# Moving four operands of VectorE from SBUF to PSUM, with three PSUM banks for the groups' sums in place of six

## The reference, cut to what matters

```python
edge_emb = edge_attr_full @ ew.T + eb
xw = x @ W
xj = xw[src].reshape(-1, H, D) + edge_emb.reshape(-1, H, D)
xi = xw[dst].reshape(-1, H, D)
alpha = einsum('ehd,hd->eh', xi, att_i) + einsum('ehd,hd->eh', xj, att_j)
alpha = leaky_relu(alpha, 0.2)
amax = segment_max(alpha, dst, num_segments=N)
ea = exp(alpha - amax[dst])
denom = segment_sum(ea, dst, num_segments=N)
msg = xj * (ea / (denom[dst] + EPS))[..., None]
h = segment_sum(msg, dst, num_segments=N).mean(axis=1) + b     # then relu, next layer
```

## Time and profile before

| | value |
|---|---|
| median of 3 runs | 3343.92 us |
| time of the profiled execution | 3336.89 us |
| its span, first to last instruction | 3335.0 us |
| mean granted clock of TensorE | 0.543 |
| busy: PE, POOL, DVE, ACT | 72%, 65%, 61%, 20% |

### The profile page before, as it was taken

One profiled execution on the slowest core, in us unless ns is written; L12 is line 12 of the kernel. 1 busy time (PEld: TensorE's weight loads), 2 busy tenths in 40 slices (PEclk: granted clock), 3 DMA queues, 4 the chain that ended last, 5 costly groups with the idle time before them and its releaser, 6 DMA issues.

```text
span 3335.0 us, 48601 instructions
## 1 busy us (share of the span) xinstructions
PE 2402.9 (72%) x13595; PEld 1979.9 (59%) x13595; DVE 2021.6 (61%) x6441; ACT 669.5 (20%) x3102; POOL 2172.8 (65%) x2357
## 2 busy tenths in 40 slices
PE   6879955777675677668477777747777685777668
PEld 6669924566564566556366565636556573556557
DVE  8965464665565565656655665755665574665557
ACT  0048921111114111110411111131111122111112
POOL 0047737777755777774677777377777737777772
PEclk9555555555557555555755555575555566555556
DMA  3211112222221222221222222122222212222221
GB/s 100 102 66 68 46 55 59 60 61 58 63 48 43 58 63 58 58 64 40 50 63 58 58 67 56 33 59 61 58 60 64 56 35 57 60 60 58 58 55 50
DMA packets 114123, 195.78 MB, mean 59 GB/s; under 512 B 39898, under 2 KB 77273, under 8 KB 113865
## 3 DMA queue, kind: packets, MB, share of 16 engines
q0 software_dynamic: 62560, 130.25, 17.4%
q1 hardware_dynamic: 51304, 62.42, 5.9%
HBM read 180.86 MB, written 11.67 MB: 58 GB/s over the span
## 4 chain that ended last, share of the span: by engine, by line
POOL 30%; DVE 28%; PE 22%; issue 13%; DMA 4%; DVEq 2%; ACT 1%; POOLq 0%; ACTq 0%
POOL ring L510 28%; PE bank L745 10%; PE bank L747 5%; DMA ring<-table,srci 4%; DVE acc L1208 2%; PE bank L718 2%; DVE into L1149 2%; PE bank L741 2%; DVE prod L1072 2%; DVE ring L847 2%; DVE lanes L1135 2%; DVE fwd L1156 1%; POOL ring L491 1%; PE bank L783 1%; DVEq L1016 1%
## 5 line engine op out<-in xcount | busy, mean ns | idle before, releaser
L510 POOL DMA_INDIRECT ring<-table,srci x1955 | 1903.9, 974 | 633.1 <-issue 571.4
L745 PE MATMUL bank<-pw,ring 128*128 128x48 f32 x3910 | 1216.9, 411 | 0.0
L745 PEld LDWEIGHTS bank<-pw,ring 128*128 128x128 f32 x3910 | 1009.1, 316 | 103.8 <-issue 23.9
L741 PE MATMUL bank<-zeros 128*128 128x288 bf16 x490 | 209.6, 428 | 622.0 <-DVE pw L1167 622.0
L747 PE MATMUL bank<-onehot,est 128*36 128x24 f32 x3910 | 619.1, 246 | 0.0
L747 PEld LDWEIGHTS bank<-onehot,est 128*36 128x36 f32 x3910 | 382.6, 150 | 177.5
L586 ACT ACTIVATE dd<-dd 128x66 f32<-128x66 f32 x75 | 19.4, 258 | 2152.2 <-DVE dd L1160 2152.2
L741 PEld LDWEIGHTS bank<-zeros 128*128 128x128 bf16 x490 | 54.3, 111 | 665.3 <-DVE pw L1167 630.7
L1111 DVE TENSOR_TENSOR alpha<-alpha,ring 128x56 f32<-128x56 f32 (+7 forms) x75 | 18.1, 241 | 702.6 <-DMA ring<-table,srci 702.4
L1208 DVE TENSOR_TENSOR acc<-acc,bank 128x288 f32 x490 | 222.4, 454 | 301.7 <-PE bank L747 183.0
L580 ACT COPY ai_win<-ai_rows 128x48 f32 x1955 | 309.1, 228 | 58.0 <-issue 22.7
(11 more groups left out here) (214 smaller groups left out, 2676.1 us busy)
## 6 DMA issues: line engine op xcount, KB each, us to landing
ring<-table,srci POOLq DMA_INDIRECT x1955
ai_rows<-lo_dram SPq DMA_DIRECT2D x28, 896.0 KB, 4.3
at<-in_attr SPq DMA_DIRECT2D x65, 224.0 KB, 2.5
table<-ring SPq DMA_DIRECT2D x15, 390.0 KB, 3.6
table<-ring SPq DMA_DIRECT2D x5, 325.0 KB, 3.3
result<-ring SPq DMA_DIRECT2D x24, 64.0 KB
x_mid<-ring SPq DMA_DIRECT2D x3, 384.0 KB, 2.7
table<-ring SPq DMA_DIRECT2D x5, 130.0 KB, 2.3
```

The lines of the kernel that those rows point to most:

```text
L510: nc.gpsimd.indirect_dma_start(out=ring[:, slot(t), :], out_offset=None, in_=table, in_offset=bass.IndirectOffsetOnAxis(ap=srci[:, t:t + 1 ...
L741: nc.tensor.matmul(total, zeros[:, 0:P], zeros[:, :], start=True, stop=False, skip_group_check=True)
L745: nc.tensor.matmul(wide[:, 0:H, at_k], ring[:, slot(t), 0:D], pw[:, g % DEEP, k, :, :], start=False, stop=False, skip_group_check=True)
```

## The change

Four operands of DVE move into PSUM, and a few instructions are merged:

- `ai_win` lies in banks 4 to 6. ACT writes it there, and DVE multiplies it in place by `onehot`, now with one TENSOR_TENSOR of 1344 elements instead of two SCALAR_TENSOR_TENSOR of 672.
- `probs`, the layer's edge vectors `v16` and the dot rows `dot_row` lie in bank 7. The products of attributes become one TENSOR_TENSOR of 896 elements each instead of two of 448. `weigh` reads `probs` instead of the copy in `est`.
- The group sums keep banks 0 to 2, `pw` has three buffers, and `AHEAD` is 3.
- The node rows at a layer's start go through bank 6 alone.
- A copy of `vrow` into `dot_row` (once a layer, after chunk 10) and one of `v17` into `v16` (at a layer's start) are added.

```diff
-AHEAD = 4
-SUM_BANKS = (0, 1, 2, 4, 5, 6)
+AHEAD = 3
+SUM_BANKS = (0, 1, 2)
...
-        bank = [ctx.enter_context(nc.psum_tensor(f"bank{i}", [P, 512], F32)) for i in range(8)]
+        banks = ctx.enter_context(nc.psum_tensor("banks", [P, 8 * 512], F32))
+        bank = [banks[:, i * 512:(i + 1) * 512] for i in range(8)]
+        ai_win = banks[:, 4 * 512:4 * 512 + K * H * WIN].rearrange("p (k h w) -> p k h w", k=K, h=H)
+        dot_row = bank[7][:, 0:H * D].rearrange("p (h f) -> p h f", h=H)
+        probs = bank[7][:, H * D:H * D + H * QB].rearrange("p (h k) -> p h k", h=H)
+        v16 = bank[7][:, H * (D + QB):H * (D + QB + FA)].rearrange("p (h f) -> p h f", h=H)
...
-                if q >= 2:
-                    pe.wait_ge(tr_sb, NQ * layer + q - 1)
+                if q >= 1:
+                    pe.wait_ge(tr_sb, NQ * layer + q)
...
-                    nc.tensor.transpose(bank[6 + q % 2][:, o:o + P], xt[:, j, 0:D], identf[:, :]).then_inc(tr_ps, 1)
+                    nc.tensor.transpose(bank[6][:, o:o + P], xt[:, j, 0:D], identf[:, :]).then_inc(tr_ps, 1)
...
+            def layer_rows(layer):
+                v.wait_ge(lay_w, 16 * 5 * (layer + 1))
+                link(V.tensor_copy(dot_row, vrow[:, :, :]))
...
-                V.tensor_tensor_reduce(out=dump[:, d % NDUMP, :], in0=xt[:, j, 0:D], in1=vrow[:, h, :], scale=1.0,
+                V.tensor_tensor_reduce(out=dump[:, d % NDUMP, :], in0=xt[:, j, 0:D], in1=dot_row[:, h, :], scale=1.0,
...
-                    for h in range(H):
-                        ins = V.scalar_tensor_tensor(out=pr[:, h, :, :], in0=at[:, gc % NAT, 0:k, :], scalar=1.0,
-                                                     in1=v17[:, layer, h, 0:FA].unsqueeze(1).broadcast_to((P, k, FA)),
-                                                     op0=ALU.mult, op1=ALU.mult)
-                    link(ins)
+                    link(V.tensor_tensor(pr, at[:, gc % NAT, 0:k, :].unsqueeze(1).broadcast_to((P, H, k, FA)),
+                                         v16.unsqueeze(2).broadcast_to((P, H, k, FA)), ALU.mult))
...
-                    for h in range(H):
-                        ins = V.scalar_tensor_tensor(out=win[:, :, h, :], in0=win[:, :, h, :], scalar=1.0,
-                                                     in1=onehot[:, ts, :], op0=ALU.mult, op1=ALU.mult)
-                    link(ins)
+                    link(V.tensor_tensor(win, win, onehot[:, ts, :].unsqueeze(2).broadcast_to((P, k, H, WIN)), ALU.mult))
...
-                                est[:, c % 2, k:k + n, HF:HF + H].unsqueeze(3).broadcast_to((P, n, H, WIN)), ALU.mult)\
+                                probs[:, :, k:k + n].rearrange("p h k -> p k h").unsqueeze(3).broadcast_to((P, n, H, WIN)),
...
-                for h in range(H):
-                    ins = V.scalar_tensor_tensor(out=es[:, :, h * FA:(h + 1) * FA], in0=at[:, gc % NAT, 0:k, :], scalar=1.0,
-                                                 in1=probs[:, h, 0:k].unsqueeze(2).broadcast_to((P, k, FA)),
-                                                 op0=ALU.mult, op1=ALU.mult)
-                ins.then_inc(est_ready, 1)
+                V.tensor_tensor(es[:, :, 0:HF].rearrange("p k (h f) -> p k h f", h=H),
+                                at[:, gc % NAT, 0:k, :].unsqueeze(2).broadcast_to((P, k, H, FA)),
+                                pr.unsqueeze(3).broadcast_to((P, k, H, FA)), ALU.mult).then_inc(est_ready, 1)
...
+                V.tensor_copy(v16, v17[:, layer, :, 0:FA])
...
+                            layer_rows(layer + 1)
```

More of the change, by code:

```diff
@@ L122, in program @@
         at = sb("at", [P, NAT, K, FA])
-        ai_win = sb("ai_win", [P, K, H, WIN])
+        w2b2 = sb("w2b2", [P, 2 * D])
         prod = sb("prod", [P, H * K * FA])
@@ L136, in program @@
         dd = sb("dd", [P, H * QB + REG])
-        probs = sb("probs", [P, H, QB])
         maxes = sb("maxes", [P, H, QB])
@@ L258, in program @@
         iota_rep = estf[:, 0:P * PC // 2].bitcast(BF16).rearrange("p (l t) -> p l t", l=P)
-        w2s = ai_win[:, :, :, :].rearrange("p k h w -> p (k h w)")[:, 0:D]
-        b2s = ai_win[:, :, :, :].rearrange("p k h w -> p (k h w)")[:, D:2 * D]
-        bank = [ctx.enter_context(nc.psum_tensor(f"bank{i}", [P, 512], F32)) for i in range(8)]
+        w2s, b2s = w2b2[:, 0:D], w2b2[:, D:2 * D]
+        banks = ctx.enter_context(nc.psum_tensor("banks", [P, 8 * 512], F32))
[4 more added lines that the diff above has]
+        v16 = bank[7][:, H * (D + QB):H * (D + QB + FA)].rearrange("p (h f) -> p h f", h=H)
         def gcn_sum(g):
@@ L599, in old_rows @@
                     nc.scalar.copy(S[:, j0:j1, D:2 * D],
-                                   bank[6 + q % 2][:, 0:(j1 - j0) * P].rearrange("p (j n) -> p j n", n=P)).then_inc(tr_sb, 1)
+                                   bank[6][:, 0:(j1 - j0) * P].rearrange("p (j n) -> p j n", n=P)).then_inc(tr_sb, 1)
                 for q in range(NQ):
@@ L1062, in _ @@
             v.sem_inc(ln_coef, 1)
-            v.wait_ge(lay_w, 16 * 5)
+            def layer_rows(layer):
+                v.wait_ge(lay_w, 16 * 5 * (layer + 1))
+                link(V.tensor_copy(dot_row, vrow[:, :, :]))
+            layer_rows(0)
             dots = [0]
@@ L1168, in weigh @@
                                 onehot[:, t:t + n, :].unsqueeze(2).broadcast_to((P, n, H, WIN)),
-                                est[:, c % 2, k:k + n, HF:HF + H].unsqueeze(3).broadcast_to((P, n, H, WIN)), ALU.mult)\
+                                probs[:, :, k:k + n].rearrange("p h k -> p k h").unsqueeze(3).broadcast_to((P, n, H, WIN)),
+                                ALU.mult)\
                     .then_inc(p_ready, 1)
@@ L1175, in chain_probs @@
                 v.wait_ge(exp_al, gc + 1)
-                link(V.transpose(probs[:, :, :], dd[:, 0:H * QB].rearrange("p (h e) -> p h e", h=H)))
+                link(V.transpose(probs, dd[:, 0:H * QB].rearrange("p (h e) -> p h e", h=H)))
                 pr = probs[:, :, 0:k].rearrange("p h k -> p k h")
@@ L1298, in _ @@
                     v.wait_ge(xmid_in, 16)
-                else:
-                    v.wait_ge(lay_w, 16 * 5 * (layer + 2))
                 for j in range(NT):
```

## The result

The changed kernel takes **3272.35 us**, the median of 4 runs (3267.82 to 3273.49), against 3344.14 us for the kernel before (4 runs): a ratio of 0.978, 95% interval 0.977 to 0.980. The forecast was 3280 us, inside a range from 3262 to 3306.

What follows compares the result with a forecast made beforehand. POOL's gathers were taken to set the pace in each layer's first 13 chunks, DVE the node phase. Gathers -54, dots -11, chain +1 gave -64 us: 3273 for the profiled execution, 3280 us as median, range 3262 to 3306.

Steps and rivals of the forecast that it cites:

- Gathers, -54: First 13 chunks of each layer: gathers no longer held beside four DVE lines, up to 58 us gained, -54 us counted.
- The 4 us allowed for new small holds: Gathers beside short two-input chain instructions (scans, maxima, sums): one hold of 0.06 us in each of 65 chunks.
- about 1.1: Sign for the gathers: none should be longer than about 1.1 us.
- Dot products, -11: Four node phases: dots no longer held beside POOL's addition, 12.5 us of holds, of which -11 us counted.
- the 27.6 that were named as a sign: Sign for the node phase: it should shrink from 30.4 to some 27.6 us.
- the 1.5 us kept for the relu: Node phases: each tile's relu must be ready for its dot, so -11 us counted of 12.5 us of holds.
- Chain, +1: Layer ends: `weigh` between scan and rows costs 0.3, merged instructions return 0.1, so 0.2 a layer, +1 us.
- Hidden work at nothing: One bank for node rows and ACT's and the added copies: counted as nothing, covered by waits for gathers.
- Rival A: PSUM operands dearer for DVE: 3323 us at half rate, 3298 with a fixed price; chance 0.10.
- Rival B: Holds stay at the changed lines, nothing gained from gathers or dots: 3345 us; chance 0.05.
- rival C: Three buffers stall PE at each group, 66 us at layer ends and 30 us in chunks: 3376 us; chance 0.05.
- rival D: New holds on a scan recur in each of 65 chunks, 26 us come back instead of 4: 3302 us; chance 0.05.

Runs made afterwards that it cites:

- run 5: Changed kernel with the destination scores `ai_win` alone back in SBUF, so the 1344-element product reads two SBUF operands: 3317.79 us, ratio 0.993.
- run 8: Changed kernel plus four unused DVE products of 672 elements a chunk in the wait for gathers, one input in PSUM: 3270.99 us.
- run 6: Changed kernel plus four unused DVE products of 672 elements a chunk in the wait for gathers, both inputs in SBUF: 3327.24 us.
- run 4: Changed kernel with the dot rows `dot_row` alone back in SBUF: 3281.28 us, ratio 0.983.
- run 2: Kernel before the change with only three sum banks and `AHEAD` 3: 3331.47 us, ratio 0.997.
- run 3: Changed kernel with each merged product split again into a pair for the two heads, operands still in PSUM: 3269.54 us, ratio 0.979.
- run 7: Changed kernel plus four unused DVE copies of 672 elements a chunk, SBUF to SBUF, in the wait for gathers: 3273.03 us.
- run 10: Changed kernel plus twelve unused 128x192 products a chunk in DVE's wait for gathers, both inputs and output in SBUF: 3271.79 us.
- run 11: Changed kernel plus twelve unused 128x192 products a chunk in DVE's wait for gathers, both inputs in SBUF, output in PSUM: 3271.49 us.
- run 1: Changed kernel with all four operands back in SBUF; merged instructions, three banks and order kept: 3383.56 us, ratio 1.013.

## Why the prediction was right

- **Gathers, -54: measured -56.5.** The step that long gathers lie beside four lines with two SBUF inputs, and that one operand in PSUM frees them, is shown by runs 5 and 8 against 6. The 4 us allowed for new small holds were too many: about 1 us lies beside the scans. The longest gather takes 1140 ns, but it is the kernel's first, with no DVE instruction beside it; the longest one beside a scan takes 1.03 us, so the "about 1.1" held.
- **Dot products, -11: measured -13.5.** Run 4 shows that they are separate from the gathers. All of the 12.5 us of holds were gained and a little more, so the node phase is 26.98 us and not the 27.6 that were named as a sign; the 1.5 us kept for the relu weren't needed.
- **Chain, +1: measured +1.4 over five layer ends.** The parts were +0.3 and -0.1 a layer; run 2 gives +0.7 for three banks with the shorter lead (73.83 to 74.52), and the merging takes back 0.3 (74.5 in run 3, 74.26 with it). Both were too small, the sum nearly right, which is in part luck. One sign was missed: PE's pitch at a layer's end stays 3.4 us, but its waits for `pw` rise from 70 to 90. In four chunks of each layer one wait of some 10 to 12 us has become two of some 3 to 6 us, which together are no longer.
- **Hidden work at nothing.** ACT's copies into PSUM turned out shorter, 197 against 228 ns in the mean; DVE's wait of 9.7 us a chunk shows the cover still there.
- **Rival A** (PSUM dearer) is out. The dots take 335 ns in the median from PSUM (332 to 345 in the other profiles) and 339 in run 4 from SBUF; L1225 takes 414 ns, 415 before. The fixed price in the Trainium skill's page "VectorE: DVE Perf Modes", section "The TRN2 errata — SBUF-src ops pay a fixed extra latency per instruction", an estimated 65 ns more for each operation moved, is not in this trace.
- **Rival B** (holds stay) falls by run 8, **rival C** (three banks stall PE) by run 2 and the layer end's 0.4 us, **rival D** (new recurring holds) by the gathers' sum. Beside the scans lie 0.8 us, and 1.2 to 2.5 us in runs 6 to 8, 10 and 11, where extra work moves the scans against the gathers; D counted 26.

The forecast lies 7.6 us above the result. 5 us of that are the sum, -64 where the span shrank by 69.0: half of it the small holds that didn't come, half the dots. 2.5 us are the step from one execution to the median: 7.0 us before, carried over, and 4.5 after. What the prediction had not seen is that the size of the old holds was partly chance: run 2 shows that a mere reordering moves them by 8 us.

## What to carry to other kernels

Where GpSimd's indirect DMAs set the pace, look for gathers longer than the median and for the VectorE instruction beside their start; if it reads two SBUF operands, put one in PSUM, the longest instruction first. Don't merge such instructions while both inputs lie in SBUF, since a hold lasts to the end of the instruction (run 1 against run 2: 54 us). And don't price a hold by a mean from another place in the order: where the gather starts in the instruction moves it between nothing and the whole.

## What the runs showed of the hardware

The hold works both ways and is set, but for some hundredths of a us, by who comes first. In run 5 a gather that starts 0.08 us into a product of 1.55 us takes 2.29 us, in run 6 one 0.20 us into a product of 0.86 us takes 1.48: both are 0.94 plus what is left of the product less some 0.12 us. If gathers started evenly over their pitch of 1.25 us, a product of length L would cost (L - 0.17)^2 / 2.5 us in the mean, an estimate from these offsets. That gives 65 x 0.76 + 5 x 0.24 = 51 us in run 5 (five layers' products of 1.55 and 0.95 us; 51.8 measured), 240 x 0.19 = 46 in run 6 (56.2) and 720 x 0.014 = 10 in run 10 (2.5). In runs 6 and 10 the starts aren't even: in run 10 nearly half of them lie at one offset.

The Trainium skill's page "SBUF — State Buffer", section "Who interferes with whom", says that a VectorE instruction with two SBUF inputs contends with a GpSimd instruction that reads SBUF, and a copy in a two-port mode with GpSimd, for a shared pair of ports, and that whoever issues first has it for the whole instruction. Runs 6 to 8 and 11 agree on the inputs and on the copy. On the order they agree in one direction: a gather waits for nearly the whole VectorE instruction, while a product that comes second waits some 0.07 us and not the gather's 0.94. Towards products, only a gather's first part counts: run 10 has 540 products that start 0.05 to 1.18 us behind a gather's start, and none takes more than 0.36 us. Towards copies a later part counts too, as run 7 shows: most copies that start 0.54 to 0.79 us behind a gather's start take some 0.17 us longer. And GpSimd's addition of 0.46 us holds a dot product that starts with it for 0.29 us. Which ports are behind this no run here shows.
